# Attention values of a head group: eight events of 256 queries become four of 512, with a second place for the turned exponentials

## The reference, cut to what matters

```python
content = jnp.einsum('bqhd,bkhd->bhqk', q + u_bias, k)
pos_score = _rel_shift(jnp.einsum('bqhd,khd->bhqk', q + v_bias, p))
attn = jax.nn.softmax((content + pos_score) / jnp.sqrt(jnp.float32(e)), axis=-1)
ctx = jnp.einsum('bhqk,bkhd->bqhd', attn, v).reshape(b, s, e)
return ctx @ Wo + bo
```

## Time and profile before

| | us |
|---|---|
| median of 3 runs | 523.55 (520.18 to 524.83) |
| the profiled execution's own time | 524.83 |
| its span in the profile | 523.0 |
| PE busy in the span | 446.3 (85%) |
| DVE, ACT, POOL busy | 358.6, 268.0, 256.2 |

### The profile page before, as it was taken

The page is one execution under the profiler, slowest core; times in us unless marked ns, Lnnn a source line. Parts: engine busy times, 40 slices in busy tenths (PEclk is TensorE's granted clock), DMA queues, the critical chain, the costliest instruction groups (busy, mean ns, idle before and its releaser), DMA issues.

```text
span 523.0 us, 9946 instructions
## 1 busy us (share of the span) xinstructions
PE 446.3 (85%) x3155; PEld 317.9 (61%) x3155; DVE 358.6 (69%) x907; ACT 268.0 (51%) x550; POOL 256.2 (49%) x272
## 2 busy tenths in 40 slices
PE   8899999999999999999777999089799797358860
PEld 7665666666767677667646999034366366247750
DVE  4987677687877787687655665566756765728872
ACT  2356567766676666766513566075444221036553
POOL 3462564457572873252143455332651664636770
PEclk9899999999999999999998999679999798559995
DMA  8499999999999900000222300640000000033205
GB/s 295 126 174 175 160 158 338 212 194 183 189 188 179 139 2 6 16 2 12 74 88 72 82 25 24 233 201 1 0 2 0 1 21 20 31 79 83 66 19 162
DMA packets 68386, 52.71 MB, mean 101 GB/s; under 512 B 3238, under 2 KB 66093, under 8 KB 67696
## 3 DMA queue, kind: packets, MB, share of 16 engines
q1 hardware_dynamic: 65360, 47.24, 46.5%
q0 software_dynamic: 2976, 4.85, 3.2%
HBM read 21.30 MB, written 32.09 MB: 102 GB/s over the span
## 4 chain that ended last, share of the span: by engine, by line
PE 66%; DVE 11%; issue 8%; POOL 5%; DMA 5%; ACT 3%; POOLq 1%; SPq 0%; DVEq 0%; ACTq 0%
PE banks L1013 13%; PE banks L1151 8%; PE banks L995 6%; PE banks L1160 6%; PE banks L1028 6%; PE banks L984 5%; PE banks L1206 3%; PE banks L990 3%; PE banks L1219 3%; PE banks L1096 2%; DVE nmax L1434 2%; DMA arena<-ct_in 2%; POOL arena L760 1%; PE banks L1143 1%; PE banks L1083 1%
## 5 line engine op out<-in xcount | busy, mean ns | idle before, releaser
L789 ACT ACTIVATE arena<-banks 128x512 f32<-128x512 f32 x128 | 76.3, 597 | 69.9 <-PE banks L1013 69.6
L782 ACT ACTIVATE work<-banks,nmax 128x512 f32<-128x512 f32 x128 | 80.7, 685 | 16.4 <-DVE nmax L1434 16.0
L1013 PE MATMUL banks<-ca,work 128*128 128x128 f32 x512 | 84.3, 288 | 3.8 <-ACT work L782 3.8
L1434 DVE TENSOR_REDUCE nmax<-banks 128x2 f32<-128x1024 f32 x64 | 78.4, 1224 | 2.2
L1013 PEld LDWEIGHTS banks<-ca,work 128*128 128x128 f32 x512 | 54.7, 142 | 36.6 <-issue 23.7
L995 PE MATMUL banks<-arena 32*128 32x512 f32 (+3 forms) x256 | 60.1, 435 | 0.0
L984 PEld LDWEIGHTS banks<-arena 32*128 32x128 f32 x256 | 41.3, 184 | 30.0 <-issue 24.5
L984 PE MATMUL banks<-arena 32*128 32x128 f32 x256 | 55.1, 295 | 0.5 <-DVE corr L1521 0.4
L1151 PE MATMUL banks<-t,arena 128*128 128x128 f32 x300 | 47.2, 295 | 3.9 <-ACT t L901 1.0
L1422 DVE COPY_PREDICATED banks<-ca,banks 128x256 f32<-128x256 uint32 x64 | 27.2, 425 | 30.0 <-PE banks L984 29.6
L1206 PE MATMUL banks<-arena 128*128 128x512 f32 x96 | 45.2, 622 | 1.2 <-POOL arena L760 1.2
(11 more groups left out here) (232 smaller groups left out, 825.5 us busy)
## 6 DMA issues: line engine op xcount, KB each, us to landing
regions<-zeros SPq DMA_DIRECT2D x15, 1040.0 KB, 18.6
regions<-zeros SPq DMA_DIRECT2D x9, 1032.0 KB, 21.9
arena<-wp_in SPq DMA_DIRECT2D x1, 4624.0 KB, 25.4
arena<-wp_in SPq DMA_DIRECT2D x1, 4494.0 KB, 16.1
arena<-ct_in SPq DMA_DIRECT2D x2, 1024.0 KB, 9.5
arena<-cb_in SPq DMA_DIRECT2D x1, 1660.0 KB, 6.9
arena<-regions SPq DMA_DIRECT2D x23, 65.0 KB, 1.9
arena<-regions SPq DMA_DIRECT2D x20, 64.5 KB, 1.9
```

Of the source, the lines that this page charges most:

```text
L782: eng.activation(prob[:, r, :], bank[r], ACT.Exp, bias=nmax[:, s % 2, jj:jj + 1]).then_inc(s_exp, 1)
L789: eng.activation(probT[:, v % 2, j0 + jj, :, i % 2 * P:(i % 2 + 1) * P], turned_in(s, jj).rearrange("p (t q) -> p t q", t=TB), ACT.Copy).t ...
L1013: mm = eng.transpose(turned_in(s, jj)[:, t * P:(t + 1) * P], prob[:, 2 * (s % 2) + jj, t * P:(t + 1) * P], ident)
L1434: eng.tensor_reduce(nmax[:, s % 2, :], pair, AX.X, ALU.max, negate=True).then_inc(count(s_fixed), 1)
```

## The change

The values of a whole group are now taken at once: `values m t` moves 512 columns, so a group has four events. They stand in the first four steps of the group that follows (steps 8 to 11, 16 to 19, and so on to 56 to 59); the other four steps of each group (4 to 7, 12 to 15, to 52 to 55) have none. Of the last group the first half stays 256 wide, four events in a row in step 60 (`half`), and the rest stays as it was (`tile`).

Since a group's turned exponentials now live for twice as long, `probT` has two places of a whole group: `arena3` for odd groups, and the first 8192 columns of `arena2` for even ones. There `wp0` comes, so SP loads it only when the values of groups 0 to 6 are done (28 events, in step 59), ahead of `cr2`.

```diff
     for s in range(STEPS):
         plan.append(("turn", s, 0))
-        if TB <= s < STEPS - TB:
-            plan.append(("values", s // TB - 1, s % TB))
-            if (s // TB - 1) % 2 == 1 and s % TB == TB - 1:
-                plan.append(("ctx", (s // TB - 1) // 2))
+        if s >= 2 * TB and s % (2 * TB) < TB:
+            plan.append(("values", s // (2 * TB) - 1, s % TB))
+            if s % TB == TB - 1:
+                plan.append(("ctx", s // (2 * TB) - 1))
         elif s == STEPS - TB:
-            plan += [("values", STEPS // TB - 2, t) for t in range(TB)]
+            plan += [("half", t) for t in range(TB)]
...
-        probT = arena3[:, :].rearrange("p (r j t q) -> p r j t q", r=2, j=HG, t=TB)
+
+        probT = [v.rearrange("p (j t q) -> p j t q", j=HG, t=TB) for v in (arena2[:, 0:HG * TB * S], arena3[:, :])]
...
-                if l == 0:
-                    eng.dma_start(wp0, wp0_in[:, :]).then_inc(s_w0, 16)
...
-            eng.wait_ge(s_pv, NHALF * TB)
+            eng.wait_ge(s_pv, LAST * TB)
+            eng.dma_start(wp0, wp0_in[:, :]).then_inc(s_w0, 16)
+            eng.wait_ge(s_pv, (LAST + 2) * TB)
             eng.dma_start(cr2, cb_in[:, WIDE_B:WIDE_B + WIDE_R]).then_inc(s_cr, 16)
...
-                    if v >= 2:
-                        eng.wait_ge(s_pv, TB * (v - 1))
+                    if m >= 2:
+                        eng.wait_ge(s_pv, TB * (m - 1))
...
-                elif kind == "values":
-                    v, t = w
-                    m, hh = divmod(v, 2)
+                elif kind in ("values", "half"):
+                    m, t = w if kind == "values" else (LAST, w[0])
+                    queried = slice(0, S if kind == "values" else S // 2)
                     b, g = divmod(m, NG)
                     if t == 0:
-                        eng.wait_ge(s_pTs, 2 * TB * (v + 1))
+                        eng.wait_ge(s_pTs, 4 * TB * (m + 1) - (2 * TB if kind == "half" else 0))
                         eng.wait_ge(*after("v", b))
-                        if m and hh == 0:
+                        if m:
                             eng.wait_ge(s_cx, m)
                     for j in range(HG):
                         h = g * HG + j
-                        mm = eng.matmul(CTX[HP * j:HP * (j + 1), 2 * P * hh:2 * P * (hh + 1)],
-                                        vv[:, b % 2, t, h * HP:(h + 1) * HP], probT[:, v % 2, j, t, :],
-                                        start=(t == 0), stop=(t == TB - 1))
+                        mm = eng.matmul(CTX[HP * j:HP * (j + 1), queried], vv[:, b % 2, t, h * HP:(h + 1) * HP],
+                                        probT[m % 2][:, j, t, queried], start=(t == 0), stop=(t == TB - 1))
```

More of the change, by code:

```diff
@@ L324, in build @@
         lg = sb("lg", [P, NTOK * E1])
+        assert HG * TB * S <= E0 * WW0
         assert WIDE_R + max(NT0, NT1) * DW1 <= 4 * TB * S
@@ L456, in turned_in @@
             return PT if jj else bank[2 * (s % 2)]
-        NHALF = STEPS // TB
+        LAST = B * NG - 1
         def place_of_step(s):
@@ L784, in _ @@
                     s, jj = w
-                    _, _, v, i, j0 = place_of_step(s)
+                    b, g, _, i, j0 = place_of_step(s)
+                    m = NG * b + g
                     eng.wait_ge(s_pT, 2 * s + jj + 1)
-                    if v >= 2:
-                        eng.wait_ge(s_pv, TB * (v - 1))
-                    eng.activation(probT[:, v % 2, j0 + jj, :, i % 2 * P:(i % 2 + 1) * P], turned_in(s, jj).rearrange("p (t q) -> p t q", t=TB),
+                    if m >= 2:
+                        eng.wait_ge(s_pv, TB * (m - 1))
+                    eng.activation(probT[m % 2][:, j0 + jj, :, i * P:(i + 1) * P], turned_in(s, jj).rearrange("p (t q) -> p t q", t=TB),
                                    ACT.Copy).then_inc(s_pTs, 1)
@@ L793, in _ @@
                     i = slice(tiles_of(w)[0] * P, (tiles_of(w)[-1] + 1) * P)
-                    eng.wait_ge(s_pv, TB * (2 * m + 1 + half_of[0] if half_of else 2 * (m + 1)))
+                    eng.wait_ge(s_pv, TB * parts(m, half_of))
                     if m:
@@ L1033, in _ @@
                     i = w[0]
-                    v, b, g = STEPS // TB - 1, B - 1, NG - 1
+                    b, g = B - 1, NG - 1
                     eng.wait_ge(s_pTs, 2 * (STEPS - TB) + 4 * (i - 1))
@@ L1040, in _ @@
                             mm = eng.matmul(CTX[HP * j:HP * (j + 1), i * P:(i + 1) * P], vv[:, b % 2, t, h * HP:(h + 1) * HP],
-                                            probT[:, v % 2, j, t, i % 2 * P:(i % 2 + 1) * P],
+                                            probT[LAST % 2][:, j, t, i * P:(i + 1) * P],
                                             start=(t == 0), stop=(t == TB - 1))
@@ L1498, in _ @@
                         if a[0] >= 2:
-                            eng.wait_ge(s_pv, (a[0] - 1) * 2 * NG * TB)
+                            eng.wait_ge(s_pv, (a[0] - 1) * NG * TB)
                         eng.wait_ge(s_vset, 2)
```

## The result

The changed kernel takes 527.82 us (median of 8 runs, 524.93 to 530.05), the kernel before beside it 523.44: a ratio of 1.009, with a 95% interval of 1.0052 to 1.0128. A second series of the same two kernels gave 526.84 against 522.56, 1.007 (1.0043 to 1.0097). So the change costs about 4 us where 0.2 of gain was forecast, and the median lies 0.3 above the range. The profiled execution took 529.13 with a span of 527.1.

A forecast was written before the change was run, and what follows sets the result against it. PE was taken to bound most steps, up to the limits of the chain of scores, the second turn and ACT. Heavy steps +11.9, light steps -12.1, sum -0.2 us: from the median 523.55 to 523.3, range 517.5 to 527.5.

The forecast's parts named there:

- in attention no clock is to be won: PE's granted clock is 9 tenths or more from the second slice to the 27th, so no gain there.
- light steps: The 28 steps that lose their values event: 0.72 us each or 20.2 on PE, 12.1 after other limits.
- Heavy steps: The 28 steps with a 512-wide values event: 0.43 us longer each, 11.9 in all after step 32's wait.
- Light steps without a late DVE: Six steps save 0.42 us each, seven 0.58, four with a 512-wide job 0.71.
- 23, 39, 14, 15 and 54: Light steps: 23 and 39 save 0.15 us each, 14 saves 0.02, 15 saves 0.4, 54 nothing.
- Steps 29 and 45: Light steps with DVE late by `xn2`, put between savings of 0.15 and 0.58: 0.4 us each.
- Steps 5: Light steps 5 and 53 save 0.58 us each, 22 and 38 save 0.71 each.
- Step 55: Light step after a long wait, without a job; PE's limit is 2.7 us: saves 0.4.
- Weights: Late load, issued by 242, takes 16.6 us, 18 to spare: costs nothing; rival that it comes late, chance 0.05.
- PE alone: Rival: the chain of scores gives way in attention; 515.3 us at full, taken as 517; chance 0.17.
- Wide events: Rival: a 512-wide values event takes two events' time, heavy steps cost 0.57 us each; 527.4 us; chance 0.08.
- The rule of the Trainium skill: Rival: weight loads overlap only where row groups differ, so eleven light steps give 0.15 us less each; 524.9; chance 0.04.

The follow-up runs named there:

- before2: The kernel before, unchanged, run again for a profile beside the second series of the changed kernel: 522.56 us.
- before3: The kernel before, unchanged, run again for its profile on a chip where it takes 537 to 541 us.
- late_w0: The kernel before with only the first experts' weights loaded as late as in the change: 537.03 us, ratio 0.9977.
- warm54: The changed kernel with three idle matmuls of 256 columns added in PE's waits of step 54: 539.61 us, ratio 0.9992.
- warm54b: The kernel of warm54 run again with more rounds: 537.27 us, ratio 1.0019.
- cover2: The kernel of cover with the idle matmuls of warm54 and the job `wo` in step 14 instead of 16: 523.68 us, ratio 1.001.
- cover3: The kernel of cover2 without idle matmuls, group 6 again in 256-wide events in steps 52 to 59, one `ctxT` a step later: 534.63 us, ratio 0.9955.
- cover3b: The kernel of cover3, unchanged, run again: 534.92 us, ratio 0.9912.
- cover3_p4: The kernel of cover3 with the late weights' load in four DMAs of a quarter of the columns each: 536.80 us, ratio 0.9922.
- late_w0b: The kernel of late_w0, unchanged, run again: 542.71 us, ratio 1.0001.
- cover: The changed kernel with values of groups 0, 2 and 4 four steps later, beside light steps, their `ctxT` jobs behind them: 542.6 us, ratio 1.0079.
- empty53: The kernel before with the four 256-wide values events of steps 52 to 55 all in step 52: 526.24 us, ratio 1.0049.
- xn2_27: The changed kernel with DVE's `xn2` one step sooner, behind that step's evacuation: 544.99 us, ratio 1.0122.
- pairs: The changed kernel with each 512-wide values event replaced by two 256-wide events in a row: 542.19 us, ratio 1.0073.
- after2: The changed kernel, unchanged, in the second series: 526.84 us, ratio 1.007.
- xn2_front: The changed kernel with `xn2` of the first two sequences moved from steps 28 and 44 to before the evacuation in 27 and 43: 538.68 us, ratio 1.0015.
- group 2: The follow-up runs before2, after2, empty53 and cover2, which shared a chip where the kernel before takes 522.6 us.

## Why the prediction was wrong

**What failed is the first step: "in attention no clock is to be won".** That was read as "none is to be lost". The light steps were costed by what the step's length loses; what PE's waits do to the clock was put at nothing and not asked. In steps 5 to 62 of the second series, at full clock, PE is busy for 206.9 us instead of 210.4, not 8 less, and idle for 7.4 instead of 2.2. Take the 18 profiles by what stands in steps 53 to 55. With values or fillers in them, ten keep the full clock from 200 to 240 (before, before2, before3, late_w0, warm54, warm54b, cover2, cover3, cover3b, cover3_p4); in the eleventh, late_w0b, it fell at 214.9, behind a step 50 of 4.5. With neither, and leaving out cover and empty53, where it fell too, three of five have a fall that begins between 228 and 234 (after, xn2_27, pairs), and two have none (after2, xn2_front). The fall costs 2.8 in after and in xn2_27 and 1.6 in pairs. What decides it in an execution the profiles don't show; late_w0b, cover3b and cover3_p4 have falls behind other waits, where values stand.

The executions without a profile say the same, since the mean granted clock of each is on record; at 525 us and two levels 0.001 less is 1 us more at half clock. The eight of after fall into two groups: four at 0.926 to 0.928 take 524.9 to 527.0, four at 0.917 to 0.921 take 528.6 to 530.1, on average 3.0 more, and the profiled one is of these. That is the size of the fall, in half of them, though where their half clock lies is not recorded. Filling the gap brought the ratio from 1.0073 (pairs) to 1.0019 (warm54b) beside each other and the median clock from 0.917 to 0.922; the intervals of the ratios just overlap, so the profiles carry this more than the ratios.

**The rest is in the sum.** Without the fall the steps cost +1.7 where -0.2 was forecast:
- Heavy steps: +11.9 forecast, and 0.42 to 0.43 each in the profile, but for 32 (0.48) and 17 (0.11); 11.7 together. Right. The reason given, that 512 columns need no more weight loads, was wrong: pairs loads twice as often in the same 1.07.
- Light steps without a late DVE (12, 20, 28 and three more at 0.42; 13, 21, 31, 37, 47 at 0.57 or 0.58; 6 and 7): right to 0.06. So were 23, 39, 14, 15 and 54.
- Steps 29 and 45: "0.4 each" saved, and 0.29 each lost: 1.4 of the 1.9. They were put between two rows by analogy, and DVE's work was not summed: from the end of the maximum that step 29 waits for (130.21) `xn2`, L1534 and L1538 last until the next score begins at 132.28. In before the same row came 0.13 before it would have set turn 30, so the 0.42 of step 28 and the 0.4 of step 29 were one saving of 0.13. xn2_front takes exactly this away.
- Steps 5 (0.23 instead of 0.58), 22 and 38 (0.54 instead of 0.71), 53 (0.46 instead of 0.58): together 0.8, of which 30 and 46 give 0.2 back.
- Step 55: 0.41 where 0.4 was forecast, when the clock holds (2.67).
- Weights: 0, right. 14.7 us instead of 16.6, issued at 244.0 without the fall and not at 242.

Of the rivals, PE alone did not bound: turn 21 waits 0.23 for an exponential. Wide events did not cost twice; that rival's 527.4 is near the time measured, by another mechanism, so its closeness is luck. The rule of the Trainium skill, "TensorE: Matmul & The Clock Gate", section "The mechanism", would make step 21 0.15 longer, 3.04; the trace has 2.89 and does not bear it out here.

**What stays open.** The medians say +4.4 and +4.3 us. The steps give 1.7, and the fall of the clock 2.8 where it comes; an estimate with a fall in every second execution is 1.4, and some 1.2 are left. They can lie between turn 63 and DVE's first copy of the experts' weights, which takes 22.1 in before and in before2 (0 and 3.4 us of it at half clock), but 23.0 in after (6.8), 24.0 in after2 (13.7, from 263.3 to 277.0) and 23.1 in cover2 (10.2). PE's busy time in the ten us ahead of 263.3 is alike in after2 and before2 (7.4 us). The kernels of before on the slower chips have the long form too (before3 23.2, late_w0b 23.9), so the change is not needed for it. But the median clock over all executions is 0.936 in before on the chip of group 2, 0.9285 in after2 and 0.926 in cover2: the changed kernels are at half clock for some 8 to 10 us more, cover2 too, which filled its gap. Where, two profiles can't tell; this is why cover2, 2.1 ahead at turn 63, was not ahead in the time. From the first copy of weights to the end these five take 242.0 to 246.5, and the shortest and the longest are both before, so one profile against one tells nothing of that part.

## What to carry to other kernels

Work that is moved off a step is a gain only up to the next limit, and the wait that then appears may not be free: look for the granted clock in more than one execution of the steps that would be left with waits, and leave some matmuls in them. Ask of each step which engine is through last before putting work there; the values of this kernel belong beside steps that DVE or the chain sets, and neither where PE is full nor where ACT's second copy is last: that placement, with `wo` and three of the `ctxT` jobs moved to fit it and group 6 left as before, turned +0.7 to +0.9% into -0.5 to -0.9%, and the width had no part in it. Not every part of it was tested alone. And where several small works of one engine meet in one step, add them up from the trace instead of taking a value between two neighbours.

## What the runs showed that was not expected

- Two 256-column events in a row (16 rows) take 1.07 us, one of 512 columns (8 rows) 1.06: the eight weight loads more cost nothing that shows.
- The same program met full clock in one execution and half for 6.8 us in another, with the same 1.06 us of PE work in the 2 us ahead (after and after2 at 228). So did the kernel of cover3 at 143.9, where the half clock lasted for 3.4 us and cost 1.6.
- In every profile on the three chips where before takes 537 to 541, ACT stood still in step 60, in that of the kernel before too (3.85 us in before3), and step 50 was 0.3 to 1.5 us longer; in no profile where before takes 523 (step 60 4.76). The clock often fell behind it (from 253.0 in before3). Its releaser is "remote"; what it waits for is open.
- Before itself takes 522.6 on one chip and 541.1 on another, 3.5% apart. Only ratios from one chip tell a change of 1%.
